# Graph network on one core: the setup merged into one program, 96-row edge loads, a table in seven chunks, and 72 gathers that read the input directly

## What is computed

```python
gathered = node_feats[node_idx]                      # x[src], one row per edge
scores = jnp.einsum('ed,d->e', gathered, W[0])
seg_max = jax.ops.segment_max(scores, he_idx, ...)   # he_idx = dst
w = jnp.exp(scores - seg_max[he_idx])
denom = jax.ops.segment_sum(w, he_idx, ...)
out = jax.ops.segment_sum((w / denom[he_idx])[:, None] * gathered, he_idx, ...)
...
x = _layernorm(x + _L0_gnn_ref(x, edge_index, 12500, L0_gnn_W))
x = _layernorm(x + _L1_gnn_ref(...))   # attention with 4 heads
x = _layernorm(x + _L2_gnn_ref(...))   # graph convolution
x = _layernorm(x + _L3_gnn_ref(...))   # edge MLP
```

## Time and profile before

| | |
|---|---|
| median of 3 runs | 8972.52 us (8969.04 to 8973.36) |
| the profiled execution | 8970.83 us, of which its span (first to last instruction) 8969.0 |
| granted TensorE clock, mean | 0.730 of 2.4 GHz |
| busiest engines | POOL 6170.7 us (69%), VectorE 5424.7 (60%), TensorE 5081.4 (57%) |
| setup, until the first gather of layer 0 | 238.1 us |
| the gathers of layer 0 and of layer 1 | 238.1 to about 2199 us, 2453 to 4440 |

### The profile page before, as it was taken

The page is one execution under the profiler, slowest core; times in us unless marked ns, Lnnn a source line. Parts: engine busy times, 40 slices in busy tenths (PEclk is TensorE's granted clock), DMA queues, the critical chain, the costliest instruction groups (busy, mean ns, idle before and its releaser), DMA issues. The chain is left out here.

```text
span 8969.0 us, 109567 instructions
## 1 busy us (share of the span) xinstructions
PE 5081.4 (57%) x27642; PEld 4066.1 (45%) x27642; DVE 5424.7 (60%) x12907; ACT 1893.9 (21%) x6410; POOL 6170.7 (69%) x6504
## 2 busy tenths in 40 slices
PE   0255555555656666666685555544456666666665
PEld 0133444444545555555553333333345555555552
DVE  3467776677777777777762222222246777777775
ACT  0000000000445555555650000000022111111115
POOL 0777777776477777777617777777745777777774
PEclk9867666666878889888895555555557787877787
DMA  2222222221455555555431111111124444444441
GB/s 71 58 54 54 54 54 54 53 54 44 140 124 123 124 123 124 123 123 124 100 98 53 53 53 53 53 53 53 53 75 132 119 119 120 119 118 119 119 117 33
DMA packets 879303, 782.06 MB, mean 87 GB/s; under 512 B 382238, under 2 KB 734070, under 8 KB 878314
## 3 DMA queue, kind: packets, MB, share of 16 engines
q0 software_dynamic: 231344, 530.60, 22.2%
q1 hardware_dynamic: 647359, 244.44, 11.1%
HBM read 713.69 MB, written 60.72 MB: 86 GB/s over the span
## 5 line engine op out<-in xcount | busy, mean ns | idle before, releaser
L777 POOL DMA_INDIRECT rows_h<-t_d,idx x3126 | 2995.5, 958 | 1199.3 <-issue 940.3
L907 PE MATMUL pn_h<-S_h,rows_h 128*128 128x128 f32 x9378 | 1821.8, 340 | 680.0 <-DVE lo_h L1103 452.7
L907 PEld LDWEIGHTS pn_h<-S_h,rows_h 128*128 128x128 f32 x9378 | 1565.1, 234 | 1000.2 <-issue 955.4
L455 POOL DMA_INDIRECT rows_mlp<-t_d,idx x1563 | 1477.9, 946 | 502.6 <-issue 476.0
L455 POOL DMA_INDIRECT rows_sum<-t_d,idx x1563 | 1475.0, 944 | 506.1 <-issue 475.9
L504 PE MATMUL pn_sum<-S_sum,rows_sum 128*128 128x128 f32 x3126 | 805.4, 439 | 971.1 <-DMA rows_sum<-t_d,idx 962.8
L504 PEld LDWEIGHTS pn_sum<-S_sum,rows_sum 128*128 128x128 f32 x3126 | 693.3, 326 | 1237.2 <-issue 1236.8
L815 ACT ACTIVATE rows_h<-rows_h,wc_h 128x64 f32<-128x64 f32 x4688 | 1134.1, 333 | 9.8
L623 DVE TENSOR_TENSOR big<-big,pn_sum 128x512 f32 x391 | 269.2, 688 | 1431.7 <-PE pn_sum L504 1431.1
L489 PE MATMUL pre_mlp<-dw_mlp,ST_mlp 128*128 128x128 f32 x3126 | 581.3, 344 | 748.6 <-DVE ST_mlp L54 735.1
L489 PEld LDWEIGHTS pre_mlp<-dw_mlp,ST_mlp 128*128 128x128 f32 x3126 | 499.8, 243 | 823.2 <-issue 822.7
(11 more groups left out here) (328 smaller groups left out, 7337.0 us busy)
## 6 DMA issues: line engine op xcount, KB each, us to landing
dw_mlp<-bd_d SPq DMA_DIRECT2D x1563, 64.0 KB
rows_h<-t_d,idx POOLq DMA_INDIRECT x3126
lrb_h<-lrrow_d SPq DMA_DIRECT2D x196, 128.0 KB
lrb_mlp<-lrrow_d SPq DMA_DIRECT2D x98, 256.0 KB, 3.5
dw_h<-xp_d SPq DMA_DIRECT2D x1563, 3.0 KB
rows_sum<-t_d,idx POOLq DMA_INDIRECT x1563
rows_mlp<-t_d,idx POOLq DMA_INDIRECT x1563
t_d<-n_tab SPq DMA_DIRECT2D x24, 522.0 KB
```

Of the source, the lines that this page charges most:

```text
L455: e.indirect_dma_start(rows[:, g % NR, j, :], None, table, bass.IndirectOffsetOnAxis(ap=idx[:, b, t:t + 1].bitcast(I32), axis=0)).then_inc ...
L777: e.indirect_dma_start(rows[:, g % NR, j, :], None, table, bass.IndirectOffsetOnAxis(ap=idx[:, b16, t:t + 1].bitcast(I32), axis=0)).then_i ...
L907: last = e.matmul(pn[g % 2][:, k, bass.ds(r0, P)], rows[:, g % NR, j, k * P:(k + 1) * P], S[:, g % NS, j, :], start=False, stop=last_tile)
```

## The change

The two setup blocks become one function, `prepare`, and a part of layer 0's gathers moves into it.

- **Edge loads.** Each array is loaded by one transfer of 96 rows (`main`) and two of a single row (`last_rows`). `src` comes first, then `dst`, `prevl` and `nextf`, then the weights. Only the tails of the last two rows are filled with padding beforehand, and the first load waits for nothing. The big scratch arrays lie in `acc`, which layer 0 uses later.
- **First gathers.** Once `src` has landed, VectorE casts it, TensorE transposes it, and VectorE copies the `idx` columns, in four quarters. POOL then issues the gathers of the first GX = 18 groups (72 tiles) straight from `x` into the ring, 128 features a row; semaphores `s_g` count them.
- **Scores of those rows.** They are computed from the gathered rows with `score`: four times 16 tiles at the end of `prepare`, and the last 8 tiles at batch 1 of layer 0.
- **Table.** ScalarE's queue loads `x` in chunks of 14 tiles into four slots in the part of the ring that the first 72 gathers don't use; chunks 4 to 6 are loaded by SP when a slot is free. VectorE scores a chunk after the edge arithmetic, SP stores it. The 44 rows that remain (and padding) go through `tail`.
- **Column copies.** `wcol`, `hi`, `lo` and `lrf` are copied out of PSUM by ScalarE, after its loads; `idx` by VectorE.
- **Registers.** The bases take their way through DRAM on ScalarE's queue.
- **Zeroing.** `acc` is zeroed in block 3 by 26 ScalarE copies of `zb`, behind the first `caps` in ScalarE's order; VectorE waits for them with `s_zero` before the first `add`.

```diff
+GX = 18
...
+        scratch = [acc[0:B, 0, k * EB:(k + 1) * EB] for k in range(6)]
+        srci, srcf, dsti, dstf, wrow, hif = scratch
...
+        def main(t, x):
+            return t[0:B - 2, :], x[0:(B - 2) * EB].rearrange("(b e) -> b e", e=EB)
+        def last_rows(e, t, x, done):
+            e.dma_start(t[B - 2:B - 1, :], x[(B - 2) * EB:full].rearrange("(b e) -> b e", b=1)).then_inc(done, 16)
+            e.dma_start(t[B - 1:B, 0:ELAST], x[full:E].rearrange("(b e) -> b e", b=1)).then_inc(done, 16)
...
+        @block.gpsimd
...
+            for g in range(GX):
+                b16, q = divmod(g, QT)
+                e.wait_ge(s_idx, q + 1)
+                for j in range(4):
+                    t = 4 * q + j
+                    e.indirect_dma_start(rows[:, g, j, 0:F], None, a["x"],
+                                         bass.IndirectOffsetOnAxis(ap=idx[:, b16, t:t + 1].bitcast(I32), axis=0)
+                                         ).then_inc(c["s_g"][g // 4], 16)
...
+            for k in range(NC):
+                x, t, n = slot(k)
+                e.wait_ge(s_sc, k + 1)
+                e.dma_start(d["t0"][t * P:(t + n) * P, :].rearrange("(t p) f -> p t f", p=P), x).then_inc(s_xo[k % 2], 16)
+                if 0 <= k - 1 < NC - 4:
+                    e.wait_ge(s_xo[(k - 1) % 2], 16 * ((k - 1) // 2 + 1))
+                    load_x(e, k + 3)
...
+        @block.scalar
...
+            for k in range(4):
+                load_x(e, k)
...
+            for k in range(4 * QT):
+                m, q = divmod(k, QT)
+                e.wait_ge(s_tp, QT + k + 1)
+                e.copy((wcol, hi, lo, lrf)[m][:, :, 4 * q:4 * q + 4], tp[k % 2][:, :, 0:B].rearrange("p t b -> p b t")).then_inc(s_ev, 1)
...
+        @block.vector
...
+            def score(x, n):
+                e.tensor_tensor(xw[:, 0:n, :], x[:, :, 0:F], wb[:, :].unsqueeze(1).broadcast_to([P, n, F]), ALU.mult)
+                e.drain()
+                e.tensor_reduce(x[:, :, F:F + 1], xw[:, 0:n, :], AX.X, ALU.add)
+                return e.drain()
...
+            for q in range(4):
+                e.wait_ge(c["s_g"][q], 16 * 16)
+                score(flat[:, 16 * q:16 * q + 16, :], 16)
...
@@ edge_soft, gpsimd
-            for g in range(GR):
+            for g in range(early, GR):
                 if g >= NR:
                     e.wait_ge(s_mm, g - NR + 1)
@@ edge_soft, scalar
+                    if b == 0 and not gat:
+                        e.wait_ge(s_init, 1)
+                        for k in range(0, RANKS, 512):
+                            n = min(512, RANKS - k)
+                            last = e.copy(acc[:, 0, k:k + n], zb[:, 0:n])
+                        last.then_inc(s_zero, 1)
@@ edge_soft, vector
-            e.memset(acc[:, :, :], 0.0)
+            if gat:
+                e.memset(acc[:, :, :], 0.0)
```

More of the change, by code:

```diff
@@ L318, in prog @@
             with nc.psum_tensor("hist", [NT, P], F32) as hist:
-                edge_soft(nc, sb, 1, t0_d, acc, hist, consts, d)
+                with ExitStack() as ring:
+                    rows = sb("rows0", [P, 32, 4, W0], F32, ring)
+                    tables = dict(wcol=wcol_d, pen=pen_d, rowpen=rowpen_d, lrrow=lrrow_d, base=base_d, rel=rel_d, qbase=qbase_d,
+                                  t0=t0_d, bd=bd_d, xp=xp_d)
+                    prepare(nc, sb, acc, rows, wn, vs, consts, a, tables)
+                    if stop <= 0:
+                        return
+                    edge_soft(nc, sb, 1, t0_d, acc, hist, dict(consts, rows=rows), d)
+                    for i in range(-(-GX // 4)):
+                        consts["landed"][i] += 16 * 4 * min(4, GX - 4 * i)
                 if debug:
@@ L667, in edge_soft @@
     fetched = [min(TB, TILES - TB * b) for b in range(NBAT)]
+    own = [n if gat else max(0, min(n, TILES - 4 * GX) if TB * b >= 4 * GX else TB * (b + 1) - 4 * GX) for b, n in enumerate(fetched)]
     PE, DVE, SP = mybir.EngineType.PE, mybir.EngineType.DVE, mybir.EngineType.SP
@@ L678, in sem @@
             return ctx.enter_context(nc.semaphore(f"{name}_h{heads}"))
-        rows = s("rows", [P, NR, 4, width])
+        rows = s("rows", [P, NR, 4, width]) if gat else c["rows"]
+        early = 0 if gat else GX
         S = s("S", [P, NS, 4, P])
@@ L725, in edge_soft @@
             ho, lo = s("ho", [P, 2, 4, NT], BF16), s("lo1", [P, 2, 4, P], BF16)
+            xw = s("xw", [P, 4 * (GX - GB), F])
+            s_zero = sem("s_zero")
         s_gb = [sem(f"s_gb{i}") for i in range(2)]
@@ L734, in landed @@
         def landed(b):
-            return s_gb[b % 2], 16 * sum(fetched[k] for k in range(b % 2, b + 1, 2))
+            return s_gb[b % 2], 16 * sum(own[k] for k in range(b % 2, b + 1, 2))
         def stage_of(i):
@@ L1132, in add @@
                 e.wait_ge(s_mm, g + 1)
+                if g == 0 and not gat:
+                    e.wait_ge(s_zero, 1)
                 if g % GB == 0:
```

413 lines of the change are left out of this document (216 added, 197 removed).

## The result

| | before | after |
|---|---|---|
| median | 8972.25 us (8969.04 to 8973.36, 4 runs) | 8768.88 us (8768.1 to 8773.84, 4 runs) |
| the profiled execution, its span | 8970.83, 8969.0 | 8768.1, 8766.3 |
| granted TensorE clock, mean | 0.730 | 0.726 |
| first gather of layer 0, the 73rd | 238.10, 328.18 | 9.22, 128.30 |
| batch 23 begins on VectorE | 2165.93 | 1962.97 |

The changed kernel takes 0.9775 of the time before, with an interval of 0.9758 to 0.9792: 203 us less. The forecast was 8749, so the kernel is faster as forecast, and 20 us short of it. The whole gain stands in the setup and the head of layer 0. From batch 23 on everything is 202 to 206 us earlier than before, and no later stage changed its length by more than 2 us.

A forecast was written before the change was run, and what follows sets the result against it. Layer 0 runs at POOL's gather-issue pace, so its start decides. With POOL issuing gather 73 at about 106, batch 23 starts 222.4 us earlier: 8970.8 − 222.4 = 8748.4, stated as 8749; range 8738 to 8795.

The forecast's parts named there:

- a late table: Setup's table stores beside gathers and loads: step 5 takes 90 us, POOL resumes at 138, 8781; 0.13 together with slow gathers.
- the rival of gathers slowed by full DMA engines: Setup's early gathers: at 1.6 us each they end at 127, time 8771; 0.13 together with the late table.
- Step 1: Edge loads: 96 rows use 16 DMA engines, 2.7 us an array, so src is usable at 8.5 us.
- Step 2: Setup's cast, transposes and idx copy: first gather at about 11.5 us, bounds 9 and 16.
- step 3: Early gathers: 72 at 1.254 us take 90.3 us, ending at 102; their scores, 4.3 us each, end hidden at 98.
- The rival "VectorE holds POOL up": Setup: six copies or casts block POOL for their length, 7 us; POOL resumes at 110.5, 8753; chance 0.09.
- Step 4: Edge arithmetic from 14 to 37 us, then the offset matmul behind 12 transpose groups; scoring starts at 39 us.
- Step 5: Table in seven chunks: first stored from 43 us, 58 us of DMA transfers, complete at 104 us.
- Step 6: Barrier at setup's end: 1.5 us after the later of 102 and 104, so gather 73 at about 106.
- Step 7: Zeroing acc in layer 0: 15 us on ScalarE, batch 0's weights perhaps 9 us later, covered by 10 us slack; no cost.
- The rows were spread: Denies the edge-load rival that 96 rows are not spread: 29 us an array, POOL resumes at 169, 8812; chance 0.04.
- Layer 1's clock: Layer 1 rival: granted clock falls from 0.87 to 0.75, adding 215 us and eating the gain; slower below that; chance 0.03.

The follow-up runs named there:

- the variant with PSUM: Changed kernel with the scores' weight row copied once to PSUM and read there by the product; second chip: 8781.31 us, ratio 0.9772 to the kernel before.
- the probe: Changed kernel plus five sorts of extra VectorE operations on scratch, during its wait for the offset matmul; 8796.72 us, one execution, second chip.

## Why the prediction was right, and where it was 20 us short

*Sign and size.* The one number on which it rested, how early POOL can work through its list, did decide: batch 23 came 203.0 us earlier and the time fell by 203. But the moment itself, POOL's 73rd gather at 98 to 116, had been given 0.70, and it came at 128.30, outside. The time lies in the range because the range was widened for a late table, which did not occur; that part is luck. By luck, too, the rival of gathers slowed by full DMA engines gave nearly the measured numbers (127, 8771): the gathers were slow, but the variant with PSUM shows another cause. The sum was 222.4. It missed the 73rd gather by 22.3 us (128.30 instead of 106) and got 2.8 us back behind it, since the 1464 gathers up to batch 23 took 1834.7 us instead of 1837.5.

*Step 1, 96 rows:* right. `src` was cast at 6.02, forecast 8.5. The share in the first 8 us was 0.71 at 192 GB/s, less than the share near 1 that was named as the sign. The variants with 96 rows in the old kernel and 97 in the new show the difference between these two counts from both sides.

*Step 2, first gather:* 9.22 instead of 11.5, inside its bounds.

*Step 3, 72 gathers in 90.3 us:* this step failed. They took 112.2 us from the first issue to the end of the last, 21.9 more. The price of a gather was taken as a mean over layer 0 in the kernel before, where VectorE's long operations beside gathers are a fill, sums that read PSUM (`acc` with `pn_h`) and comparisons with `iop_h`, which lies in PSUM too. The setup's products and its scan have both inputs in SBUF. Only short ones of that kind had run beside a gather, and the trace of before shows what they do, VectorE and POOL:

```profile
405.62 0.42 DVE L968 TENSOR_TENSOR_SCAN g_h<-pen_h,f_h 64x128 f32<-64x128 f32 x1
405.67 1.12 POOL L777 DMA_INDIRECT rows_h<-t_d,idx  x1 [0.30 <-issue]
```

Of the gathers from 239 to 700 us in that trace, eleven take 1.02 to 1.12 us, and every one of them stands beside such a scan of 0.41 to 0.48 us. In a mean of 0.948 they can't be seen.

The rival "VectorE holds POOL up" had the right mechanism, but it counted only copies and casts, at 7 us. Gathers that began beside those lost about 2.7 of the 22.4 us; the rest began beside operations with two SBUF inputs. 13.0 us of the excess lie after 45 us, where besides one cast only scores run, and the variant with PSUM took them away. The other 9.4, beside the edge arithmetic, were not changed by any run and are put down to these two causes by their rows and the probe's. The bound that was missing: each product of the scores (seven of 2.0 and four of 2.3 us) and each step of two SBUF inputs in the edge arithmetic (three of 2.3 us, the scan of 4.4) holds at most one gather for at most its length, 34.5 us in all.

The other half of step 3, that the scores of the gathered rows are hidden, failed too but cost nothing by itself. VectorE's last score ended at 116.75, not at 98: the four scores stand behind all chunk scores, which end at 93.8, and take 4.7 us each (two operations of 2.29, and no overlap) with a wait of 2.5 (112.06 is the start of the last). In the changed kernel POOL was later still. As soon as POOL was faster it became the limit, in both variants with the weight row in PSUM.

*Step 4, scoring starts at 39:* it started at 48.40. VectorE waited 13.36 us for `offp`. In TensorE's order, the offset matmul stands behind the transposes, as forecast, but those stood behind the matmuls for `pv`, which waited until 34.61 for `a2`. That load is ScalarE's eighth issue, behind four chunks of x whose issue took 17.22 us. I had worked out when ScalarE was free but not who waited for the last of its loads.

*Step 5, table at 104:* the moment is right (104.6), by two errors that cancel. The first store was issued at 52.58, 9 us later than forecast, and from there it took 52 us, not 60. Stores and loads had a share of 1.16 and 1.23 at 180 and 231 GB/s, so the 58 us of transfer that I had allowed was more than they needed beside the gathers. The rival of the late table did not come about on this chip.

*Step 6, the barrier costs 1.5 us:* this failed too. It was priced by a block in which POOL had issued nothing. Behind 72 gathers the wait on POOL's queue takes 6.86 us. Forecast were 4.2 us between the last gather (101.8) and the 73rd, for the table, so the difference is 2.7 us. Together: −2.3 (step 2) + 21.9 (step 3) + 2.7 (step 6) = 22.3.

*Step 7, zeroing on ScalarE:* right. The 26 copies lie between 131.32 and 144.67; batch 0 waited for its exponentials, and batch 1's rows still came later than VectorE was ready (it waited 10.8 us for them). Rows of ScalarE, then of VectorE:

```profile
131.32 13.35 ACT L893 CAST acc<-zb_h 128x512 f32<-128x512 bf16 x26
```

```profile
199.54 1.23 DVE L1057 TENSOR_TENSOR xw_h<-rows,wb 128x1024 f32<-128x1024 f32 x1 [10.77 <-DMA rows<-t_d,idx]
```

*The other rivals.* The rows were spread. POOL's waits for matmuls in layer 0 were 10 of at most 0.3 us (6 before), and no stage behind layer 0 changed its length by more than 2 us, so neither of the signs against the forecast came to anything. Layer 1's clock stayed (0.88 between 2500 and 3300, 0.87 before) with 630 gathers in 800 us as before.

## What to carry to other kernels

A price read from one stage holds beside the same kinds of operations only, and a mean hides what a few of them do: before work is moved, list what each engine's neighbours read and write there, and bound those that no row shows. When indirect DMAs move into a block, its end costs a wait on POOL's queue (6.9 us here), and an operand in PSUM instead of SBUF lets GpSimd go on beside VectorE. After a limit is taken away, look up who is last next before you count the gain: here three of them (gathers, the end of the block, VectorE's last score) lay within 12 us.

## What was not expected of the hardware

- An indirect gather that begins beside a product of two SBUF tiles ends only after it (2.16 us beside one of 2.29, where 0.94 is usual), and so it is with a scan (4.66 beside 4.42). A gather that is under way when the product begins is not lengthened, and with one input in PSUM none is.
- On two of four chips ScalarE and VectorE went on about 20 us after the TensorE result that they waited for, while GpSimd issued gathers (21 and 26 us in two rows, at a granted clock of 1.00), and the kernel before took 10459 and 10545 us instead of 8972.
- A block in which POOL has issued indirect gathers lets the next gather go 6.86 us after the end of the last of them, and without the wait on POOL's queue the next gather follows at once (1.25 us from start to start).
